# One fused adaLN block, float32 on one core: attention of both batches moved ahead of the feed-forward loop

## What is computed

```
mod = (silu(c) @ wmod).reshape(2, 6, 1, -1)      # sa, ca, ga, sb, cb, gb
ga, gb: sign kept, size raised to at least 0.25
h = layernorm(x) * (1 + ca) + sa
x = x + ga * (h @ (weight where its 32x32 block of mask is on).T + bias)
h = layernorm(x) * (1 + cb) + sb
x = x + gb * ffn(h)
ffn(h) = lora2(silu(lora1(h)) * lora3(h)),  lora(x) = x @ w.T + 2 * (x @ a.T) @ b.T
```

## Time and profile before

| | us |
|---|---|
| median of 3 runs | 302.51 (302.38 to 302.60) |
| span of the profiled execution, first to last instruction | 303.3 |
| busy: PE / DVE / ACT / POOL | 263.6 / 135.3 / 85.7 / 55.6 |
| first matmul of step 0 | 59.73 |
| from 190 on: PE busy without a gap, until 297.4 | 107.4 |

### The profile page before, as it was taken

How to read it: one execution, slowest core, us unless ns; L and a number is a source line. 1 busy time by engine, 2 the same in 40 slices (tenths; PEclk the granted TensorE clock), 3 DMA queues, 4 the chain that set the end, 5 groups by cost and what they waited for, 6 DMA issues and landing times.

```text
span 303.3 us, 3130 instructions
## 1 busy us (share of the span) xinstructions
PE 263.6 (87%) x1105; PEld 193.9 (64%) x1105; DVE 135.3 (45%) x225; ACT 85.7 (28%) x163; POOL 55.6 (18%) x80
## 2 busy tenths in 40 slices
PE   0799938914969999999995999999999999999992
PEld 0425523704738778787773777678888888888771
DVE  2846369911848556483741754315511011111126
ACT  1139303801314542524310658201111101110110
POOL 1401184113133135141311153000000000000003
PEclk9999968775989999999999599999999999999998
DMA  7999300510212320311300320000300000000003
GB/s 282 400 375 408 152 0 5 205 35 0 71 39 101 104 71 3 101 47 60 104 0 0 121 89 0 2 0 16 123 2 1 0 2 0 0 0 2 0 1 138
DMA packets 9619, 23.20 MB, mean 76 GB/s; under 512 B 1154, under 2 KB 1410, under 8 KB 9220
## 3 DMA queue, kind: packets, MB, share of 16 engines
q1 hardware_dynamic: 9168, 22.86, 21.1%
q10 hardware_dynamic: 436, 0.14, 0.2%
HBM read 20.90 MB, written 2.10 MB: 76 GB/s over the span
## 4 chain that ended last, share of the span: by engine, by line
PE 66%; issue 5%; DVE 2%; POOL 1%; ACT 1%; POOLq 0%; DVEq 0%; ACTq 0%
PE up_b L864 18%; PE up_a L864 18%; PE acc L878 7%; PE acc L880 7%; PE acc L879 7%; PE side L828 4%; PE side L842 2%; PE side L847 1%; PE side L788 1%; ACT work L452 1%; DVE work L636 1%; PE side L820 1%; DVE xt L640 0%; POOL ht_lo L339 0%; POOL b L352 0%
## 5 line engine op out<-in xcount | busy, mean ns | idle before, releaser
L747 DVE TENSOR_TENSOR g<-up_b,g 128x512 f32<-128x512 f32 (+1 forms) x22 | 15.2, 690 | 71.9 <-PE up_b L864 71.8
L525 ACT ACTIVATE g<-up_a 128x512 f32<-128x512 f32 (+1 forms) x22 | 13.1, 598 | 87.1 <-PE up_a L864 87.0
L620 DVE SCALAR_TENSOR_TENSOR raw<-side,raw 128x512 f32<-128x512 f32 (+2 forms) x33 | 21.6, 678 | 34.9 <-PE side L842 27.3
L878 PE MATMUL acc<-w_hi,g_hi 128*128 128x512 f32 (+1 forms) x88 | 36.7, 417 | 0.0
L880 PE MATMUL acc<-w_hi,g_lo 128*128 128x512 f32 (+1 forms) x88 | 35.7, 406 | 0.0
L879 PE MATMUL acc<-w_lo,g_hi 128*128 128x512 f32 (+1 forms) x88 | 35.7, 406 | 0.0
L864 PE MATMUL up_a<-ht_lo,w_hi 128*128 128x512 f32 (+1 forms) x88 | 25.1, 409 | 10.5 <-POOL ht_lo L339 10.5
L470 ACT ACTIVATE w_hi<-raw 128x512 fp32r<-128x512 f32 (+2 forms) x33 | 20.2, 626 | 45.1 <-DVE raw L620 45.1
L530 ACT ACTIVATE g_hi<-g 128x512 fp32r<-128x512 f32 (+1 forms) x22 | 13.9, 632 | 53.1 <-DVE g L747 53.1
L375 POOL TENSOR_TENSOR xt<-work,xt 128x512 f32<-128x512 f32 x5 | 6.3, 1266 | 115.6 <-DVE work L636 108.4
L864 PEld LDWEIGHTS up_a<-ht_lo,w_hi 128*128 128x128 f32 (+1 forms) x88 | 16.8, 192 | 15.2 <-POOL ht_lo L339 10.9
(11 more groups left out here) (86 smaller groups left out, 348.4 us busy)
## 6 DMA issues: line engine op xcount, KB each, us to landing
raw<-in_ffn SPq DMA_DIRECT2D x33, 256.0 KB, 2.7
wmod_sb<-in_wmod SPq DMA_DIRECT2D x4, 768.0 KB, 14.3
xt<-in_x SPq DMA_DIRECT2D x2, 1024.0 KB, 5.1
wmod_sb<-in_wmod SPq DMA_DIRECT2D x4, 512.0 KB, 9.4
out<-xt SPq DMA_DIRECT2D x8, 256.0 KB, 2.4
mask_sb<-in_mask SPq DMA_DIRECT2D x1, 1024.0 KB, 7.3
wmod_sb<-in_wmod SPq DMA_DIRECT2D x1, 1024.0 KB, 12.7
wa<-in_weight SPq DMA_DIRECT2D x4, 256.0 KB, 13.8
```

What stands on the lines that cost most here:

```text
L525: nc.scalar.activation(g[0:w], up_a[0:w], ACT.Silu).then_inc(silu_ready, 1)
L620: nc.vector.scalar_tensor_tensor(w, side[SIDE[("merge", r)] % 2][0:rows, 0:cols], SCALING, w, ALU.mult, ALU.add).then_inc(merged, 1)
L747: nc.vector.tensor_tensor(g[0:w], up_b[0:w], g[0:w], ALU.mult).then_inc(g_ready, 1)
L878: nc.tensor.matmul(acc[t][:], hi, down_hi[j][0:w], start=(j == 0), stop=False)
```

## The change

- **Order.** Attention of both batches stands ahead of the feed-forward loop. `STEP_ATTN` is gone; of the norms only those of batch 1's feed-forward are left inside the loop (`STEP_TURN`, steps 3 to 6).
- **Chunks.** The first 12 norms are turned by chunks of 128 features and all 512 rows (`turn(q)`), so that a chunk fills one bank. `modulate(q)` on ACT writes the rounded chunk and the exact chunk in two passes of 128x512; the exact one goes to `hbuf`, two buffers, and the second pass waits for `low(q - 2)`. `attention(b, k)` adds one chunk of features to all four `acc` banks.
- **Attention's end.** `attn_gate` on DVE writes to `mid`, two buffers, so tile `n` waits for the addition of tile `n - 2`; six of the eight additions are POOL's. Batch 1's attention uses the same `acc` banks, so its bias product for tile `t` waits for `attn_gated` of batch 0.
- **Gates.** Made in half rows, 256 numbers in each of four partitions; `spread_gates` does two broadcasts of 128x256 for each of the four rows, into a single `gate_row`.
- **`b13`** has one copy: `spread(j)` waits for the merges of slice `j - 1`.
- **Mask** and attention weight are loaded, summed and masked chunk by chunk; `x` comes in tiles; the order of loads is new; 10 warm matmuls stand at the very start instead of 16 ahead of step 0.

The core of the diff (POOL's, DVE's and ACT's lists are told by the rows of the next section; the new functions of the mask and the vectors only cut the old ones in four):

```diff
 NB = D // BLOCK
+HALF = D // 2
...
-WARM_MATMULS = 16
+WARM_MATMULS = 10
...
+PASSES = [(0, 0), (1, 0), (0, 1), (1, 1)]
...
+CHUNKS = 12
+LOW_DVE = (5, 7, 9, 11)
+X1_POOL = (0, 2, 4, 5, 6, 7)
+X2_POOL = (0, 1, 2, T, T + 2)
+STEP_TURN = {3: 0, 4: 1, 5: 2, 6: 3}
...
-POOL_ADDS = {"x1": (0, 1, 2), "x2": (T, T + 2)}
...
+            load_x(0)
+            load_attention(0)
             for k in range(KT):
                 sp.dma_start(wmod_sb[:, k, 0:GATE_A * D], wmod_rows[:, k, 0:GATE_A * D]).then_inc(wmod_a_loaded[k], 16)
-            gate_cols = slice(GATE_A * D, SHIFT_F * D)
-            sp.dma_start(wmod_sb[:, :, gate_cols], wmod_rows[:, :, gate_cols]).then_inc(wmod_gate_loaded, 16)
-            for k in range(KT):
-                sp.dma_start(wa[:, k], weight[:, k]).then_inc(wa_loaded[k], 16)
-            def load_lora(n):
-                lo, hi = LORA_CUTS[n]
-                sp.dma_start(lora_raw[:, lo:hi], lora[:, lo:hi]).then_inc(lora_loaded[n], 16)
+            for k in range(1, KT):
+                load_attention(k)
+            load_x(1)
+            load_mod(GATE_A, SHIFT_F, wmod_ga_loaded)
             for n in range(LORA_EARLY):
                 load_lora(n)
-            for k in range(KT):
-                sp.dma_start(wmod_sb[:, k, SHIFT_F * D:], wmod_rows[:, k, SHIFT_F * D:]).then_inc(wmod_f_loaded[k], 16)
+            load_mod(SHIFT_F, GATE_F, wmod_f_loaded)
             for r in range(3 * HT):
                 if r == 3:
+                    load_mod(GATE_F, GATE_F + 1, wmod_gf_loaded)
+                elif r == 4:
                     for n in range(LORA_EARLY, len(LORA_CUTS)):
                         load_lora(n)
-                elif r == 5:
-                    sp.dma_start(xt[:, 1], x_rows[1]).then_inc(x_loaded[1], 16)
                 if r >= SLOTS:
 
                     sp.wait_ge(w_ready, r - SLOTS + 1)
                 sp.dma_start(raw[:, r % SLOTS], ffn[r]).then_inc(raw_loaded[r % SLOTS], 16)
...
+            def low(q):
+                i, k = divmod(q, KT)
+                b, _ = PASSES[i]
+                pool.wait_ge(high_ready, q + 1)
+                if q < CHUNKS:
+                    pool.wait_ge(h_ready, q + 1)
+                    src, tile = hbuf[:, q % 2], (slice(None), k)
+                else:
+                    src = work[:, k].rearrange("p (k s) -> p k s", k=KT)
+                    tile = (slice(None), slice(None), slice(k * P, (k + 1) * P))
+                nc.gpsimd.tensor_tensor(ht_lo[b][tile], src, f32(ht_hi[b][tile]), ALU.subtract
+                                        ).then_inc(low_by_pool, 1)
...
             def spread(j):
                 w = WIDTH[j]
                 pool.wait_ge(parts_ready, LORA_EARLY if j < 2 else len(LORA_CUTS))
                 pool.wait_ge(half_on_ready, 1)
-                if j >= 2:
-                    pool.wait_ge(merge_out, 3 * (j - 2) + 2)
+                if j:
+                    pool.wait_ge(merge_out, 3 * (j - 1) + 2)
                 for n in range(2):
-                    nc.gpsimd.tensor_scalar(b13[j % 2][:, n, 0:w],
-                                            f32(parts[:, LORA_B13 + j * P:LORA_B13 + j * P + w]), factors[:, 1 + n:2 + n],
-                                            None, ALU.mult).then_inc(b13_ready, 1)
...
+            def spread_gates(n, b, ended):
+                pool.wait_ge(*ended)
+                pool.wait_ge(gates_ready, n + 1)
+                if b or n:
+                    pool.wait_ge(*((down_gated, T) if n and b else (attn_gated, T * (B * n + b))))
+                for half in range(2):
+                    row = (2 * b + half) * QUAD
+                    nc.gpsimd.partition_broadcast(gate_row[:, half * HALF:(half + 1) * HALF],
+                                                  (gates_a, gates_f)[n][row:row + 1]).then_inc(gate_row_ready, 1)
+                    pool.wait_ge(gate_row_ready, 2 * (B * n + b) + half + 1)
+            def add_x1(n):
                 b, t = divmod(n, T)
-                pool.wait_ge(gated, n + 1)
-                nc.gpsimd.tensor_tensor(xt[:, b, t], work[:, t], xt[:, b, t], ALU.add
-                                        ).then_inc(rows_added[x, "pool"], 1)
+                pool.wait_ge(attn_gated, n + 1)
+                nc.gpsimd.tensor_tensor(xt[:, b, t], mid[:, n % 2], xt[:, b, t], ALU.add).then_inc(x1_by_pool, 1)
...
+            def modulate(q):
+                i, k = divmod(q, KT)
+                b, second = PASSES[i]
+                act.wait_ge(turned, q + 1)
                 act.wait_ge(cols_ready, second + 1)
-                src = side[SIDE[("norm", i)] % 2] if i >= TILES else acc[i % T]
+                if second:
+                    act.wait_ge(attn_out, T * (b + 1))
+                src = turn_bank(q)
+                scale, bias_col = one_plus[:, second, k, b:b + 1], shift[:, second, k, b:b + 1]
+                nc.scalar.activation(ht_hi[b][:, k], src[:], ACT.Identity, bias=bias_col, scale=scale
+                                     ).then_inc(high_ready, 1)
+                if q >= 2:
+                    act.wait_ge(*low_done(q - 2))
+                nc.scalar.activation(hbuf[:, q % 2], src[:], ACT.Identity, bias=bias_col, scale=scale
+                                     ).then_inc(h_ready, 1)
...
+            def attn_gate(n):
+                b, t = divmod(n, T)
+                dve.wait_ge(attn_out, n + 1)
+                dve.wait_ge(gate_row_ready, 2 * (b + 1))
+                if n >= 2:
+                    dve.wait_ge(*x1_done(n - 2))
+                nc.vector.tensor_tensor(mid[:, n % 2], acc[t][:], gate_row[:], ALU.mult).then_inc(attn_gated, 1)
...
+                    moment(12)
+                    moment(13)
+                    norm(12)
+                    moment(14)
+                    norm(13)
+                elif s == 2:
+                    moment(15)
+                    norm(14)
+                    norm(15)
                 if s == HT:
                     for n in range(T):
                         down_end(n)
...
+            def turn(q):
+                i, k = divmod(q, KT)
+                pe.wait_ge(normed, T * (i + 1))
+                if i < 2:
+                    if q >= 3:
+                        pe.wait_ge(h_ready, q - 2)
+                elif q == 2 * KT:
+                    pe.wait_ge(h_ready, 2 * KT - 2)
+                elif q == 2 * KT + 1:
+                    pe.wait_ge(cols_ready, 2)
+                else:
+                    pe.wait_ge(h_ready, q - 1)
+                dst = turn_bank(q)
+                for t in range(T):
+                    last = nc.tensor.transpose(dst[:, t * P:(t + 1) * P], work[:, t, k * P:(k + 1) * P], ident[:])
+                last.then_inc(turned, 1)
+            def turn_tile(t):
+                dst = free_side(("turn", t))
+                pe.wait_ge(normed, 3 * T + t + 1)
                 for k in range(KT):
-                    last = nc.tensor.transpose(dst[:, k * P:(k + 1) * P], work[:, i % WORK, k * P:(k + 1) * P],
-                                               ident[:])
+                    last = nc.tensor.transpose(dst[:, k * P:(k + 1) * P], work[:, t, k * P:(k + 1) * P], ident[:])
                 last.then_inc(turned, 1)
...
+            def attention(b, k):
+                if k == 0:
+                    for t in range(T):
+                        if b:
+                            pe.wait_ge(attn_gated, t + 1)
+                        nc.tensor.matmul(acc[t][:], ones[:], bias_parts[:], start=True, stop=False)
+                pe.wait_ge(high_ready, KT * b + k + 1)
+                if b == 0:
+                    pe.wait_ge(wa_high_ready, k + 1)
+                if k == KT - 1:
+                    if b == 0:
+                        pe.wait_ge(wa_ready, k + 1)
+                    pe.wait_ge(*low_done(KT * b + k))
+                    for t in range(T):
+                        tile = slice(t * P, (t + 1) * P)
+                        nc.tensor.matmul(acc[t][:], ht_hi[b][:, k, tile], wa_hi[k][:], start=False, stop=False)
+                        nc.tensor.matmul(acc[t][:], ht_hi[b][:, k, tile], wa_lo[k][:], start=False, stop=False)
+                        nc.tensor.matmul(acc[t][:], ht_lo[b][:, k, tile], wa_hi[k][:], start=False, stop=True
+                                         ).then_inc(attn_out, 1)
+                    return
+                for t in range(T):
+                    nc.tensor.matmul(acc[t][:], ht_hi[b][:, k, t * P:(t + 1) * P], wa_hi[k][:], start=False, stop=False)
+                if b == 0:
+                    pe.wait_ge(wa_ready, k + 1)
+                for t in range(T):
+                    nc.tensor.matmul(acc[t][:], ht_hi[b][:, k, t * P:(t + 1) * P], wa_lo[k][:], start=False, stop=False)
+                pe.wait_ge(*low_done(KT * b + k))
+                for t in range(T):
+                    nc.tensor.matmul(acc[t][:], ht_lo[b][:, k, t * P:(t + 1) * P], wa_hi[k][:], start=False, stop=False)
...
```

(80 more changed lines are left out.)

703 lines of the change are left out of this document (337 added, 366 removed).

## The result

The changed kernel takes 321.24 us (median of 4 runs, 318.95 to 324.33), the kernel before 302.56 beside it: ratio 1.060, 95% interval [1.0545, 1.0647]. Slower, as predicted, but by 18.7 us and not by 8.5, and outside the range. The ratio leaves out the 324.33, a slow run. The profiled execution took 320.73 us, its span is 318.7.

What follows compares the result with a forecast made beforehand. TensorE, busy 87% of the span, was taken as the bound, with its main waits ending on POOL or DVE. Hinge at 107.4 plus 204.4 behind it made 311.8, less 0.8: 311.0 us, range 302 to 318.

Steps and rivals of the forecast that it cites:

- the hinge: merge(6), the first TensorE product that needs spread(2): at 87.2 us before, forecast at 107.4, 20.2 later.
- POOL's list ahead of the hinge: POOL's work up to spread(2), with three passes of 14.2 us each, puts the hinge at 107.4 us.
- Pass ends: A pass is a group of gate-row broadcasts with POOL's idle time before and behind; ends forecast at 50.4, 81.3, 106.1.
- What is added behind it: After the hinge: b13 waits in steps 4 to 7 +8.4, steps 2 and 3 +1.5, half clock +0.8 us.
- the wait of 4.2: In the kernel before, TensorE's wait at 163 to 167 us; 3.1 us of half clock counted after it.
- Behind the hinge: Old 216.1 us after the hinge, less 22.4 for batch 1's attention, turns, a wait and its half clock: 193.7.
- 0.8 of clock: Just after the hinge: a longer pause, 8 us, costs 2.5 of half clock instead of 1.7, so +0.8 us.
- Less the 0.8 by which the span exceeds the median: Last step of the sum, span to time: 311.8 us less 0.8 gives 311.0.
- PE and DVE at the hinge: Rival: PE and DVE, not POOL, set the hinge, at 99.5; time 299.1 us; 11%.
- The waits that do not come: Rival: no waits for b13 in steps 4 to 7; 302.6 us, no change; 6%.
- Passes at the upper rows: Rival: the three passes ahead of the hinge take 16.6 us each, 2.4 more; 318.2 us; 9%.
- The rule weighed: Skill's section alone: code load ahead of broadcasts, none behind, each pass 7.2 us; 290 in all; 2%.

Runs made afterwards that it cites:

- Run 5: The changed kernel with only the third pass of broadcasts, spread_gates(1, 0), moved behind spread(10) in POOL's list: 310.66 us, ratio 1.021.
- Run 11: The changed kernel with spread(3) and spread(4) ahead of the roots and spread(5) to spread(8) ahead of the lows in POOL's list: 300.0 us, ratio 0.989.
- run 2: The changed kernel with eight extra unread matmuls just ahead of TensorE's wait for b13 in steps 4 to 7: 314.17 us, ratio 1.035.
- run 9: The changed kernel with POOL's list mended, gate rows spread by TensorE and ACT, and unread matmuls ahead of three early waits: 276.83 us, ratio 0.915.
- run 1: The changed kernel with spread(5) to spread(8) moved ahead of low(12) to low(15) in POOL's list: 305.01 us, ratio 1.008.

## Why the prediction was right in its direction and wrong in its size

The error is 321.24 - 311.0 = 10.2 us: 0.9 at the hinge, 6.0 behind it (318.7 - 108.34 = 210.4 against 204.4), 2.8 from span to time (+2.0 and not -0.8), and 0.5 by which the median lies above the profiled execution.

- **POOL's list ahead of the hinge: right.** Pass ends 50.4, 81.3 and 106.1 were to be; they came at 49.68, 81.22 and 106.99. Hinge 107.4, measured 108.34, with TensorE waiting 9.4 us (about 8), released by `b`. Step 0 starts at 83.34 (83.5). Run 5 shows that this hinge counts one to one. One sign came smaller: TensorE waits 8.67 us ahead of the bias of tile 2 and 1.14 ahead of that of tile 0, not about 12 at once.
- **"What is added behind it": the step that failed.** Waits and half clock in steps 2 to 7 were +8.4 and +1.5, in all 9.9. Run 11, in which none of them is left, shows 21.2 in the time, and 20.5 in the spans behind the hinge (210.4 against 189.9), so the term was 10.6 us too small. The four waits of steps 4 to 7 were sized right, 8.25 measured against 8.4. But I priced half clock only behind the waits of 3 to 9 us, by the earlier trace rows and the wait of 4.2, and nothing behind those of 2: four times none, where run 2 shows 6.3 us together in the lengths of the steps, 7.1 in the time. The waits of steps 2 and 3 were 2.45 and 1.07 against 1.1 and 0.4, with half clock behind the first as well.
- **"Behind the hinge", 193.7 and 0.8 of clock: 4.6 us too much, which hid part of it.** Run 11 has no waits behind its hinge, and 295.9 - 106.02 = 189.9 us there. Most of the 4.6 is a piece of the change that neither the list of changes nor the sum has: the third merge of each slice read 64 partitions before and reads all 128 now. The kernel before, then the changed one:

```profile
136.54 0.40 PE L880 MATMUL acc<-w_hi,g_lo 128*128 128x512 f32 x1
136.86 0.49 PE L847 MATMUL side<-parts 64*128 64x512 f32 x1
137.28 0.49 PE L878 MATMUL acc<-w_hi,g_hi 128*128 128x512 f32 x1
137.61 0.40 PE L879 MATMUL acc<-w_lo,g_hi 128*128 128x512 f32 x1
```
```profile
135.07 0.40 PE L930 MATMUL acc<-w_hi,g_lo 128*128 128x512 f32 x1
135.30 0.40 PE L900 MATMUL side<-parts 128*128 128x512 f32 x1
135.54 0.40 PE L928 MATMUL acc<-w_hi,g_hi 128*128 128x512 f32 x1
135.77 0.39 PE L929 MATMUL acc<-w_lo,g_hi 128*128 128x512 f32 x1
```

  From the first to the fourth start it is 1.07 us before and 0.70 now, 0.37 less in each of the nine steps behind the hinge, some 3.3. A turn ahead of attention's bias took 0.53 us (138.78 to 139.31) where one ahead of `up_a` takes 0.36: three times 0.17, 0.5. A step with attention shows both: it takes 13.34 us before (129.29 to 142.63), one of run 11 with its turned tile 9.53 (129.80 to 139.33), 3.8 less and not the 3.32 of attention's own rows. And the 0.8 did not come: from the hinge to the next `up_a` it is 5.46 us before, behind a wait of 2.98, and 5.26 in run 11 and 5.02 in the change, behind waits of 9.3 and 9.4. So a longer pause did not cost more half clock here.
- **"Less the 0.8 by which the span exceeds the median": wrong.** In all four runs of the changed kernel the time is the span plus 2.0; in every later run of the kernel before it is the span plus 1.8 (302.38 with a span of 300.6). So the profiled execution of before, with its span of 303.3, was by this estimate one of some 305.1, near the top of the 301.3 to 306.0 over all its runs, and I set my sum of spans against a median that belongs to shorter ones. The 0.2% that I gave one measurement was too narrow as well: the intervals of the runs are 0.4 to 0.7% wide on each side.
- **The rivals.** PE and DVE at the hinge: did not come, its time 299.1 (its sum left out the 1.5 of steps 2 and 3; with them it is 300.6). The waits that do not come: no. Passes at the upper rows: no, they took 14.1 to 14.8 while nothing was loaded. None of them had the mechanism that decided, clock lost behind short waits.
- **The rule weighed**, a load only ahead of the broadcast: the trace shows 7.1 to 7.5 us behind each pair, and the 290 it would have given was not near.

The deeper mistake is one of reading. I saw that the change lengthens the way to the hinge by 20 us and takes 22 us out of the steps, and treated the four waits as small change. They were the result: with those six calls moved, the rest of the change is about even (0.989 of before).

## What to carry to other kernels

On an engine that runs its list in order, put what a later engine waits for ahead of what only has to be done some time; here six moved calls were worth 21 us, and no instruction was added. Price a short wait on TensorE twice: its length, and the matmuls behind it at half clock; where it can't be removed, matmuls that nobody reads give the clock back, as run 2 and run 9 show. And where an engine shows long idle time named `issue` around one kind of operation, replace the operation: a product with a column of the identity and a copy took 1.9 us in place of 13.6, and gave 27 us in the kernel before, the fastest result here together with the changed order, its list mended and its early waits filled (277.0 and 276.8).

## What the hardware showed that I had not expected

- Half clock behind waits of 2.06 us: the matmuls behind such a wait are slow in steps 4 to 7 and in step 2, and filling the wait cured it. It does not come each time. In run 1 a wait of 2.54 us is followed by full clock, and in run 5 one of 3.57; the wait of 1.07 in step 3 was too. What decides it these runs do not show. The row of run 1:

```profile
120.44 0.71 PE L896 MATMUL side<-b,parts 128*128 128x256 f32 x4 [2.54 <-POOL b L350]
120.99 1.09 PE L915 MATMUL up_b<-ht_hi,w_hi 128*128 128x512 f32 x4
```

- Two broadcasts of half a row, 0.60 us each, with one idle time ahead and one behind: what is paid is the way to the broadcasts and the way back, not the broadcast. Between `low`, `spread`, `root` and the additions no such idle time stands in the rows.
- A DMA that reads one partition 128 times is slow: 8.7 us of VectorE's wait, 11.2 from issue to use. The half rows, 128 KB each, land 6.9 to 11.1 us after their issue, and the two at 216 us, where no weights are loaded, in 8.9 (median), whereas the 256 KB tiles of weights land in 2.7 us in the same kernel.
- A product out of 64 partitions between products out of 128 cost 0.37 us more than one out of all 128: the starts of the four rows above are 0.32, 0.42 and 0.33 us apart before, 0.23, 0.24 and 0.23 now. Why, these runs do not show.
